# Spreading a batch's neighbour scores over the rows through DRAM instead of by TensorE

## What is computed

```python
Wh = einsum('bnd,od->bno', layernorm(x), W)
ei, ej = Wh @ a1, Wh @ a2
e = ei[:, :, None] + ej[:, None, :]
e = where(e > 0, e, 0.2 * e)
e = where(adj == 0, -inf, e)
x = x + einsum('bij,bjo->bio', softmax(e), Wh)
x = x + gated_experts(layernorm(x))
```

## Time and profile before

| | |
|---|---|
| median of 3 runs | 2808.19 us (2808.19 to 2808.91) |
| the profiled execution | 2809.31 us |
| its span, first to last instruction | 2807.4 us |
| PE busy | 2774.5 us, 99% |
| DVE busy | 2413.1 us, 86% |
| ACT busy | 2106.8 us, 75% |
| mean granted TensorE clock | 0.998 |

### The profile page before, as it was taken

One profiled execution on the slowest core, in us unless ns is written; L12 is line 12 of the kernel. 1 busy time (PEld: TensorE's weight loads), 2 busy tenths in 40 slices (PEclk: granted clock), 3 DMA queues, 4 the chain that ended last, 5 costly groups with the idle time before them and its releaser, 6 DMA issues.

```text
span 2807.4 us, 46140 instructions
## 1 busy us (share of the span) xinstructions
PE 2774.5 (99%) x17114; PEld 2469.6 (88%) x17114; DVE 2413.1 (86%) x3408; ACT 2106.8 (75%) x2832; POOL 487.5 (17%) x707
## 2 busy tenths in 40 slices
PE   8999999999999999999999999999999999999998
PEld 7999999998788888888888888888888888888887
DVE  8999999997888888888888888888888888888887
ACT  7889889887777777777777777777777777777775
POOL 4555555555000000000000000000000000001000
PEclk9999999999999999999999999999999999999999
DMA  4455555543455554545445455545545554545554
GB/s 163 154 167 163 157 166 162 162 153 119 139 170 165 161 166 154 165 156 161 163 155 165 154 165 161 165 153 170 157 163 157 160 164 154 166 154 163 153 162 145
DMA packets 160060, 445.91 MB, mean 159 GB/s; under 512 B 16032, under 2 KB 73800, under 8 KB 159840
## 3 DMA queue, kind: packets, MB, share of 16 engines
q1 hardware_dynamic: 159840, 442.98, 50.2%
HBM read 401.99 MB, written 40.93 MB: 158 GB/s over the span
## 4 chain that ended last, share of the span: by engine, by line
PE 74%; DVE 1%; ACT 0%; issue 0%; DMA 0%; DVEq 0%; ACTq 0%
PE head_ps L53 12%; PE head_ps L55 12%; PE head_ps L54 12%; PE m_ps L1284 7%; PE m_ps L1287 7%; PE m_ps L1286 7%; PE z_ps L55 4%; PE z_ps L53 4%; PE z_ps L54 4%; PE turn_ps L1257 1%; PE turn_ps L1265 1%; DVE h_lo L1569 0%; DVE h_sums L1576 0%; DMA wo_ops<-wo_scratch 0%; ACT h_hi L1432 0%
## 5 line engine op out<-in xcount | busy, mean ns | idle before, releaser
L1416 ACT ACTIVATE h<-head_ps,bn_shift,bn_scale 128x512 f32<-128x512 f32 x768 | 593.9, 774 | 532.5 <-PE head_ps L55 319.9
L1569 DVE TENSOR_TENSOR h_lo<-h_sums,h_hi 128x1792 fp32r<-128x1792 f32 (+1 forms) x257 | 518.2, 2017 | 199.9 <-ACT h_hi L1432 199.8
L1432 ACT ACTIVATE h_hi<-h_sums 128x1792 fp32r<-128x1792 f32 (+1 forms) x257 | 435.4, 1694 | 63.6 <-DVE h_sums L1589 58.0
L1576 DVE TENSOR_TENSOR h_sums<-h,gate_row 128x1024 f32<-128x1024 f32 x256 | 313.7, 1225 | 114.5 <-ACT h L1416 96.7
L87 POOL TENSOR_TENSOR ffn_vareps<-ffn_mv,ln_eps 128x4 f32<-128x4 f32 x32 | 7.1, 223 | 1860.4 <-DVE ffn_mv L81 1860.4
L1536 DVE TENSOR_TENSOR h_lo<-h,h_hi 128x1024 fp32r<-128x1024 f32 x256 | 311.9, 1218 | 6.8 <-ACT h_hi L1446 6.8
L53 PE MATMUL attn_ps<-wh_hi,pT_hi 128*128 128x256 f32 x1024 | 304.9, 298 | 0.0
L54 PE MATMUL attn_ps<-wh_lo,pT_hi 128*128 128x256 f32 x1024 | 287.9, 281 | 0.0
L55 PE MATMUL attn_ps<-wh_hi,pT_lo 128*128 128x256 f32 x1024 | 287.8, 281 | 0.0
L1446 ACT ACTIVATE h_hi<-h 128x1024 fp32r<-128x1024 f32 x256 | 270.9, 1058 | 0.1
L1284 PE MATMUL m_ps<-h_hi,wo_ops 128*128 128x256 f32 x896 | 256.0, 286 | 3.1 <-DMA wo_ops<-wo_scratch 3.1
(11 more groups left out here) (215 smaller groups left out, 7619.3 us busy)
## 6 DMA issues: line engine op xcount, KB each, us to landing
wh_lo<-wo_scratch SPq DMA_DIRECT2D x124, 896.0 KB, 6.4
wo_ops<-wo_scratch SPq DMA_DIRECT2D x124, 896.0 KB, 6.5
adj_sb<-in_adj SPq DMA_DIRECT2D x128, 512.0 KB, 3.5
gate_row<-w_scratch SPq DMA_DIRECT2D x256, 256.0 KB, 4.6
x_sb<-in_x SPq DMA_DIRECT2D x64, 256.0 KB, 2.9
x_scratch<-x_sb SPq DMA_DIRECT2D x128, 128.0 KB, 1.8
ffn_x<-x_scratch SPq DMA_DIRECT2D x16, 512.0 KB, 7.6
x_sb<-x_scratch SPq DMA_DIRECT2D x16, 512.0 KB, 7.5
```

The costliest lines, as they stand in the source:

```text
L1416: return act.activation(dst, src, ACT.Relu, bias=bn_shift[layer][:, col], scale=bn_scale[layer][:, col])
L1432: act.activation(h2_hi[s % 2][:, a:b, :], g2[:, 1 + a:1 + b, :], ACT.Copy) \
L1569: dve.tensor_tensor(h2_lo[s % 2][:, a:b, :], g2[:, 1 + a:1 + b, :], bits(h2_hi[s % 2][:, a:b, :]), ALU.subtract).then_inc(S["h2_lo_ready"], 1)
L1576: dve.tensor_tensor(h2_rows, h2[:, :, :], gate[s % 2][:, :].unsqueeze(1).to_broadcast([P, KB, BANK]), ALU.mult).then_inc(S["gated_ready"], 1)
```

## The change

For batches 1 to 15 the spread is taken from PE, ACT and DVE. A DRAM scratch tensor `ej_scratch` of two rows of 1024 numbers is added. At the head of slots 2 and 10 SP waits for the last `wh_lo` of the new batch, stores the score column from `e_cols` with two DMAs (each writes 512 single elements of 4 bytes: even and odd tiles have their columns swapped), waits until both have landed, and loads the row with `partition_broadcast` into all 128 rows of `ej_rows`. The factor `-EDGE_UNIT` is moved into `a_sb` at the start, once. The head of the batch after no longer waits for the copies out of `head_ps`. The first mask of a new batch (t = 8 and t = 16) leaves slots 2 and 10 and becomes the first DVE instruction of slots 3 and 11, where it waits for the load. The other masks stay where they are.

```diff
+            def spread_ej(b, i):
+                sp.wait_ge(S["wh_lo_ready"], b * TB + TB)
+                for c in range(2):
+                    sp.dma_start(ej_dram[i].rearrange("(j c p) -> c p j", c=2, p=P)[c], e_cols[i][:, 1 - c:TB:2, 1],
+                                 allow_slow_non_contiguous=True).then_inc(ej_stored, DMA)
+                sp.wait_ge(ej_stored, 2 * DMA * b)
+                sp.dma_start(ej_rows[i][:, :], ej_dram[i].partition_broadcast(P)).then_inc(ej_in[i], DMA)
+
             def slot(k, u, last):
+                head = head_at(k, u, last)
+                if head and head[1] == HEADS + 1:
+                    spread_ej(2 * k + head[0], head[0] % 2)
...
                 if j == 0:
-                    wait(pe, S["ej_left_ready"], b)
-                    wait(pe, S["ej_right_ready"], b)
+                    wait(pe, S["wh_lo_ready"], b * TB)
...
                 head = head_at(k, u, last_pair)
-                if head and head[1] == HEADS + 1:
-                    b = 2 * k + head[0]
-                    spread_ej(b, head[0] % 2, head_ps, S["wh_lo_ready"], b * TB + TB)
...
-                if head and head[1] == HEADS + 1:
-                    head_ej(2 * k + head[0], head[0] % 2)
...
+            dve.tensor_scalar(a_sb[:, :, 1], a_sb[:, :, 1], -EDGE_UNIT, None, ALU.mult) \
+                .then_inc(S["a_scaled"], 1)
...
+            def mask(k, t, n):
...
+                if b == 0:
+                    dve.wait_ge(S["ej_left_ready"], 1)
+                    dve.wait_ge(S["ej_right_ready"], 1)
+                elif t % TB == 0:
+                    dve.wait_ge(ej_in[b % 2], DMA * ((b + 1) // 2))
+                wait(dve, S["pT_ready"], n - 4)
+                dve.scalar_tensor_tensor(scores[t % 4][:, 0:N], adj_sb[t % 2][:, :], 0.0, ej_rows[parity(t)][:, :],
+                                         ALU.is_equal, ALU.add).then_inc(S["masked_ready"], 1)
             def slot(k, u, last):
+                ok, t, n = tile_at(k, u, 5, last)
+                if ok and t % TB == 0 and not (k == 0 and t == 0):
+                    mask(k, t, n)
...
                 ok, t, n = tile_at(k, u, 6, last)
-                if head and step == HEADS + 1:
-                    head_ej(hb, hi)
-                if ok:
...
+                if ok and (t == 0 and k == 0 or t % TB):
+                    mask(k, t, n)
```

More of the change, by code:

```diff
@@ L355, in attention_block @@
         gates = Gates(*gate_parts, *gate_rows, br_sb, sem, "gate0")
+        ej_dram = nc.dram_tensor("ej_scratch", [2, N], FP32, kind="Internal").ap()
+        ej_stored, ej_in = sem("ej_stored"), [sem(f"ej_in{i}") for i in range(2)]
         small_in = sem("small_in")
@@ L727, in _ @@
             pe.wait_ge(S["w_centred_ready"], 1)
-            pe.wait_ge(S["a_scaled"], 1)
+            pe.wait_ge(S["a_scaled"], 2)
             weigh_ej()
@@ L770, in head_ej @@
                 act.wait_ge(S["ej_rows_psum"], 2 * b + 1)
-                rows = (head_ps if b else attn_ps)[:, 0, :]
-                act.activation(ej_rows[i][:, 0:BANK], rows, ACT.Copy, scale=-EDGE_UNIT) \
+                act.activation(ej_rows[i][:, 0:BANK], attn_ps[:, 0, :], ACT.Copy) \
                     .then_inc(S["ej_left_ready"], 1)
@@ L929, in head_ej @@
                 dve.wait_ge(S["ej_rows_psum"], 2 * b + 2)
-                rows = (head_ps if b else attn_ps)[:, 1, :]
-                dve.tensor_scalar(ej_rows[i][:, BANK:N], rows, -EDGE_UNIT, None, ALU.mult) \
+                dve.tensor_copy(ej_rows[i][:, BANK:N], attn_ps[:, 1, :]) \
                     .then_inc(S["ej_right_ready"], 1)
+            def mask(k, t, n):
+                if k == 0 and t in (2, 3):
+                    dve.wait_ge(S["wh_ready"], 4 * (t - 1))
+                dve.wait_ge(adj_in[t % 2], DMA * (k * (UT // 2) + (t // 2 + 1)))
+                b = 2 * k + t // TB
+                if b == 0:
[6 more added lines that the diff above has]
+                                         ALU.is_equal, ALU.add).then_inc(S["masked_ready"], 1)
             def slot(k, u, last):
+                ok, t, n = tile_at(k, u, 5, last)
+                if ok and t % TB == 0 and not (k == 0 and t == 0):
+                    mask(k, t, n)
                 head = head_at(k, u, last)
```

## The result

The changed kernel takes 2979.65 us (2976.22 to 2980.25), 6.1% more than before: the ratio is 1.0608, with an interval of 1.0589 to 1.0627. The forecast of 2852 had the right sign, but the loss is 171 us and not 44, and the time lies outside the range given.

What follows compares the result with a forecast made beforehand. DVE was taken as the bound from each batch's first mask on. 15 x (2.45 us wait + 0.5 clock) = 44 us, plus 0.1, gave 2852 us against the median of 2808.2; range of 8 in 10: 2818 to 2892.

Steps and rivals of the forecast that it cites:

- What bounds the kernel: Attention stage: from a batch's first mask, for over five of eight slots, DVE bounds; PE's freed 0.87 us is worth nothing.
- Rival E: Attention stage: PE's queue sets the batch, each giving back up to 0.87 us, 2795 us; chance 0.06.
- The idle time for `pT_hi`: DVE before `pT_lo`: x1 done at 259.89, then a wait for `pT_hi` until 261.2, using up the freed 0.7 us.
- The store: SP's two 4-byte stores per batch: landing 2.7 us after issue, upper end 3.1, taken from the `a_sb` load.
- Rival C: Stores to DRAM: 4-byte writes take twice what reads do, 5.4 us; wait 5.15 per batch, 2897 us; chance 0.11.
- The load: Broadcast load of the row into 128 rows: lands 3.5 us after issue, 4.7 as the high bound.
- The wait goes into the time one for one: First mask of 15 batches: DVE waits 2.45 us for the row, and nothing after it absorbs this.
- the order that I gave: Behind the mask: ReLU, `pT_hi`, square, exponential on ACT, then PE's next transposes at mask start + 4.95 us.
- The clock: PE's gap of nearly 4 us after the mask's slot: clock falls in two batches of three, 0.5 us per batch.
- rival B: PE clock falls to its low level in every batch, 1.7 us each with none covered, 2870 us; chance 0.14.
- SP's loads: Loads that SP issues late have over a slot of room; tile 10's mask lands by 270, wanted at about 272.

Runs made afterwards that it cites:

- free kernel: Changed kernel without the stores and the load, masks of batches 1 to 15 reading the row of batch 0: 2811.4 us, ratio 1.0011.
- load-only kernel: Changed kernel with the row stored to DRAM only once, at batch 1, and the broadcast load kept for every batch: 2822.9 us, ratio 1.0055.
- kernel with rows: Changed kernel with two small PE transposes, a DVE copy and a store of 4 rows of 1 KB replacing the 4-byte stores: 2866.0 us, ratio 1.0203.
- filled kernel: Changed kernel with 20 unneeded matmuls in PE's gap ahead of the next probability transposes: 2975.3 us.
- store-only kernel: Changed kernel with its stores and SP's wait but no load, masks reading the row of batch 0 without waiting: 2900.2 us.
- padded kernel with 512 B: Load-only kernel plus, in every batch, two awaited stores of 512 4-byte elements, each element in its own 512 B line: 2864.0 us.

## Why the prediction was right and wrong

**What bounds the kernel: right, as far as the runs go.** The free kernel fits that from the first mask on the batch goes by DVE's order. It shows that neither PE's 0.87 us nor DVE's 0.7 is worth anything once the mask has moved: 40.7 us per batch before and after. Rival E falls with it. The idle time for `pT_hi` that I worked out, 1.3 us, is 1.39 in the row at 319.30.

**The store: the step that failed.** The forecast's mechanism, a wait for the row at 15 first masks that nothing absorbs, was right, and so was its sign. The store's term in the sum was mis-sized. I took 2.7 us for its landing from the loads of `a_sb`, 3.2 us from first issue to the load's issue, with 3.1 as the upper end of the landing. It is 10.0, which is 6.8 us per batch or 102 us in all. The row was of 4-byte reads from DRAM, and I let it stand for 4-byte writes to DRAM because the piece had the same size. The other row, the store of 16 KB, was a write, but in long pieces; a store in that shape did take 1.25 us. Neither row had both properties, so their span was no bound. Rival C named the right thing and gave the stores twice the reads' time, 5.4 us; counted from the second store's issue, as I had counted, the landing is about 9.5 us, 3.5 times. A case that no row bounds should have had no upper end from rows, and the range should have been open there.

The sentence of the Trainium skill that I weighed (DMA: Bandwidth & Descriptors, Specifications) spoke against these stores: below 512 B the DMA engine does a read-modify-write. The runs agree with its direction: the store of 1 KB pieces has a way of 1.25 us, that of 4-byte pieces at least 2.35. Pieces between 4 B and 1 KB were not tried, so 512 B as the bound isn't tested here. And small pieces alone don't explain the loss: 1024 elements of 4 B with 512 B from one to the next take 2.4 to 2.9 us, no more than I had assumed. At 32 B from one to the next sixteen elements share 512 B, and it is still only 3.0 to 3.8. It is the close neighbourhood of the writes that makes them three to four times slower.

**The load: a little low.** 3.5 us taken, 4.4 median measured, 0.9 per batch or 13 us. Its longest, 5.8 us, is above the upper bound of 4.7 that I took from the mask loads, and within the row of the gates' broadcast, 3.3 to 6.0. In the load-only kernel, without the stores ahead of it, the median is 3.7.

**The wait goes into the time one for one: right.** 6.8 + 0.9 more than the forecast 2.45 is 10.2 us, and the rows show 10.3. From one batch's stores to the next's it is 52.1 us on average, 11.4 more than the 40.7 before, and 15 times that is the 171. ACT's wait follows by 11.02 and PE's by 11.07, in the order that I gave, and the transposes start 4.99 us after the mask (335.87 - 330.88), where I had 4.95.

**The clock: falls more often than I said, at a small price.** I had a fall in two batches of three and 0.5 us per batch for it. The clock fell in all 15, behind gaps of 11 us and not of 4; in the kernel with rows, where PE's gaps are about 4 us, it fell in 13 of 15. In this rival B was nearer. In the batch shown PE worked some 3.6 us at the half level, with 6 or 7 matmuls in each us instead of 10 to 12, which costs it about 1.8 us, close to my 1.7. Rival B's price of 1.7 us uncovered falls, as all that is left beyond the waits is 1.2 per batch. The filled kernel points to 0.55 to 0.7, but doesn't resolve it.

**SP's loads: right for the forecast's stores, wrong for these, without effect.** I wrote that they had over a slot of room. (The "tile 10" there is the third tile of the new batch.) With the standstill of 11 us they don't: the store-only kernel takes 89 us more than the free kernel. With the standstill of about 3 us of the forecast they have: in the padded kernel with 512 B DVE has no wait for `adj_sb`, and 44.6 of its 56 us are waits for the row.

**Left open.** Beyond the waits for the row (154.0) 17.5 us of the 171 remain. Some 3 of them are also in the free kernel, and by the estimate above 8 to 11 are the clock. The rest isn't placed. The kernel with rows has 13 us beyond its waits too, and the padded one with 512 B 11. Nor did any run tell how writes of 8 or 16 B behave.

## What to carry to other kernels

A price for a DMA is a price for its direction, its piece size and its layout together: a row of reads doesn't bound writes, and neighbouring 4-byte writes to DRAM took 8.8 to 11.1 us where the same number spread out took 2.4 to 2.9. Turning the column into rows on the chip before the store brought that to 1.25 to 1.7 us, though the detour as a whole still lost 2%. And before work is moved off an engine, run the kernel with that work left out altogether: here the ceiling was 7 us of 2808, and the mask's later place alone cost 10.

## What the runs showed of the hardware that I had not expected

Stores of 1024 elements of 4 B to neighbouring addresses complete 8.8 to 11.1 us after their first issue, though the last piece leaves the DMA engines 1.8 us after it. An instruction load of 16 KB that ran in the time between took up to 4.0 us, where it takes at most 1.7 in the attention stage before. Half as many elements take 7.8 to 9.4, so the time doesn't go with their number. 32 B from one element to the next bring it to 3.0 to 3.8 us, 64 B to 2.5 to 3.4. Four pieces of 1 KB took 1.25 us in most batches. A broadcast load of one 4 KB row into 128 rows landed in 3.7 to 5.8 us, median 4.4, behind the slow stores, against 3.6 median for a load of 512 KB of different data in the same kernel. Without the stores ahead of it, in the load-only kernel, its median is 3.7.
